# Layer 0 context attention: probabilities turned on VectorE, contexts in row quarters, queries through head queries

## The reference

```
q = split_heads(x @ Wq) * 64 ** -0.5         # 16 heads of 64
k, v = split_heads(context @ Wkv)            # 257 keys a batch, and one null key for all
attn = softmax(q @ k.T)                      # 32 tokens x 258 keys for each batch and head
out = (attn @ v) @ Wout                      # 4096 x 128
out = layernorm(out) * ln_scale + ln_bias ; x = x + out
```

## Time and profile before

| | |
|---|---|
| median of three runs | 4478.43 us |
| span of the profiled execution | 4472.7 us |
| start of the first `scores` / end of the stage's last instruction | 66.47 us / 1493.06 us |
| TensorE busy over the span | 3820.3 us, 85% |
| VectorE / ScalarE / GpSimd busy over the span | 62% / 45% / 18% |

### The profile page before, as it was taken

How to read it: one execution, slowest core, us unless ns; L and a number is a source line. 1 busy time by engine, 2 the same in 40 slices (tenths; PEclk the granted TensorE clock), 3 DMA queues, 4 the chain that set the end, 5 groups by cost and what they waited for, 6 DMA issues and landing times. The chain is left out here.

```text
span 4472.7 us, 86385 instructions
## 1 busy us (share of the span) xinstructions
PE 3820.3 (85%) x31654; PEld 2744.1 (61%) x31654; DVE 2761.5 (62%) x5370; ACT 2025.9 (45%) x4334; POOL 816.0 (18%) x797
## 2 busy tenths in 40 slices
PE   8999999999999772389998779899997777879776
PEld 6777777777777441266676356566664345656454
DVE  5666666666666586522224866577776946878683
ACT  2333333333333455444333344388887745644323
POOL 0000000000000131200000046555552022200160
PEclk9999999999999886789999889999998989989868
DMA  3111111111111055410000032222220000000000
GB/s 110 49 48 48 48 48 48 48 48 48 48 48 53 14 153 163 148 39 0 0 0 26 1 134 114 99 63 68 68 72 23 0 6 3 0 13 0 9 2 24
DMA packets 202958, 216.01 MB, mean 48 GB/s; under 512 B 37280, under 2 KB 190784, under 8 KB 195280
## 3 DMA queue, kind: packets, MB, share of 16 engines
q1 hardware_dynamic: 202704, 212.63, 15.0%
HBM read 185.26 MB, written 27.05 MB: 47 GB/s over the span
## 5 line engine op out<-in xcount | busy, mean ns | idle before, releaser
L3944 PE MATMUL c_psO<-c_pt,c_vc 128*128 128x512 f32 x1024 | 485.5, 596 | 2.5 <-ACT c_ot L4053 2.5
L3916 PE MATMUL c_psS<-c_kc,c_qt 128*128 128x257 f32 x2048 | 465.9, 380 | 1.1 <-DVE c_qt L4092 1.1
L4045 ACT ACTIVATE c_sc<-c_psS,c_mx 128x257 f32<-128x257 f32 x512 | 214.9, 472 | 487.0 <-DVE c_mx L4110 487.0
L3916 PEld LDWEIGHTS c_psS<-c_kc,c_qt 128*128 128x128 f32 x2048 | 381.2, 190 | 67.0 <-issue 17.5
L637 PEld LDWEIGHTS f_psY<-f_w_down,f_hT 128*128 128x128 f32 x2560 | 302.7, 192 | 64.3 <-issue 48.4
L680 ACT ACTIVATE f_hT<-f_psH,f_b_up 128x512 f32<-128x512 f32 x320 | 214.2, 688 | 279.6 <-PE f_psH L627 274.6
L3901 PEld LDWEIGHTS c_psQ<-XT,c_m 128*128 128x128 f32 x1984 | 258.6, 191 | 96.3 <-issue 92.3
L627 PE MATMUL f_psH<-f_xs,f_w_up 128*128 128x512 f32 x640 | 301.7, 607 | 17.6 <-ACT f_hT L680 17.6
L637 PE MATMUL f_psY<-f_w_down,f_hT 128*128 128x128 f32 x2560 | 306.9, 276 | 9.7 <-ACT f_hT L680 5.2
L2320 POOL TENSOR_TENSOR x_sc<-x_sc,x_rec 128x1156 f32<-128x1156 f32 x128 | 270.5, 2113 | 208.4 <-DVE x_rec L2586 208.4
L4053 ACT ACTIVATE c_ot<-c_psO 128x512 f32<-128x512 f32 x256 | 152.9, 597 | 342.6 <-PE c_psO L3944 342.6
(11 more groups left out here) (819 smaller groups left out, 7687.1 us busy)
## 6 DMA issues: line engine op xcount, KB each, us to landing
c_kc<-in_ctxT SPq DMA_DIRECT2D x128, 257.0 KB
c_vc<-in_ctx SPq DMA_DIRECT2D x128, 256.0 KB
g_wide<-g_w_dram SPq DMA_DIRECT2D x32, 1024.0 KB, 8.3
x_kc<-in_ctxT SPq DMA_DIRECT2D x32, 512.0 KB
x_vc<-in_ctx SPq DMA_DIRECT2D x64, 256.0 KB
l_k_dram<-l_dist SPq DMA_DIRECT2D x32, 256.0 KB, 4.0
l_q_dram<-l_turn SPq DMA_DIRECT2D x8, 1024.0 KB, 9.8
y_pt<-l_q_dram SPq DMA_DIRECT2D x8, 1024.0 KB, 6.5
```

Of the source, the lines that this page charges most:

```text
L3916: mm = pe.matmul(psS[:, r, 0:KEYS], qt[:, b // BT, half, b % BT, r * G:(r + 1) * G].rearrange("p h i -> p (h i)"), kc[:, b // 2 % 2, b % 2 ...
L3944: mm = pe.matmul(psO[:], vc[:, slot, c % 2, t, half * P:(half + 1) * P], pt[:, c % 2, t], start=(t == 0), stop=(t == 1))
L4045: act.activation(sc[:, b % 2, r, 0:KEYS], psS[:, r, 0:KEYS], ACT.Exp, bias=mx[:, b % 2, r:r + 1]).then_inc(exp_done, 1)
```

## The change

Four things are altered together:

1. The probabilities are turned by VectorE, with one STREAM_TRANSPOSE of 128 x 1024 (`scale_and_turn`), which turns each 32 x 32 block in its place. The four tokens-by-head quarters of the partitions stay apart, and the keys come to lie 32 to a quarter. The eight TensorE transposes and their two readouts go.
2. The contexts are formed in four row quarters: 64 products of 32 rows, 128 columns each (before 4 of 128 rows, 512 columns), each quarter into a bank of its own. The values of a batch must lie in all four quarters, so they are loaded four times (`values`, 4 DMAs of 256 KB for each batch). S and V read two banks each. The contexts now run one batch behind the scores instead of two.
3. The queries are formed in two steps. `heads` makes head queries (two products of 128 x 128 a batch), S takes them out into `c_qh`, and `fill` multiplies them with the key weights in two row halves of 64 (eight products of 128 columns a batch) into the score banks, right after the exponentials have been taken. S and V read two banks each. `c_m` is not formed any more.
4. The banks are now `c_psA` (scores, queries) and `c_psB` (contexts, head values, head queries, output). `head_values` is spread over four batches, `output` comes one group later, and `att` takes the place of the tokens in `XT`. The loads of `context_weights` are reordered, and the counting of x (bn_stats) moves behind its steps.

```diff
+                def fill(banks, j):
+                    for half in range(2):
+                        for a in range(2):
+                            for e in range(2):
+                                mm = pe.matmul(banks[:, 2 * a + e, half * P:(half + 1) * P],
+                                               w["k"][e * DV:(e + 1) * DV, 2 * j + a, half * P:(half + 1) * P],
+                                               qh[e * DV:(e + 1) * DV, 2 * j + a], start=True, stop=True)
+                    mm.then_inc(q_in, 1)
...
-                def turn(n, b):
-                    pe.wait_ge(scaled, n + 1)
...
+                def context(n, b, count, valued, heads_read, outs_read, opening=False):
+                    pe.wait_ge(turned, n + 1)
+                    pe.wait_ge(vc_loaded[b % 4], count * 64)
+                    pe.wait_ge(heads_ready, heads_read)
...
+                    for half in range(2):
+                        for t in range(KB):
+                            for e in range(G):
+                                mm = pe.matmul(psB[:, e, half * P:(half + 1) * P],
+                                               vc[e * S:(e + 1) * S, b % 4, t, half * P:(half + 1) * P],
+                                               pt[e * S:(e + 1) * S, :, t], start=(t == 0), stop=(t == KB - 1))
...
+                        scores(i, b, first, last)
...
+                        if not (last and s == 1):
+                            pe.wait_ge(heads_ready, n + 2)
+                            pe.wait_ge(exp_done, n * EX + G)
+                            pe.nop(nofuse=True)
+                            fill(psA, b % BT)
+                        if not (first and b == 0):
+                            pe.wait_ge(ot_ready["act"], n)
...
+                            head_values(psB[:, 1], 1 - s, b % BT)
+                        if b % BT == 0 and not first:
+                            output(m - 2, s)
...
+                            heads(psB[:, 0], i * 2 + (b + 1) // BT + 1, (2 * to, 2 * to + 1))
...
+                def scale_and_turn(n, b, first):
+                    v.wait_ge(rec_done, n + 1)
+                    v.tensor_tensor(sc[:, b % 2], sc[:, b % 2], bcast(rc[:, b % 2], 2, NK), ALU.mult)\
+                        .then_inc(scaled, 1)
+                    v.wait_ge(scaled, n + 1)
+                    if not (first and b == 0):
+                        v.wait_ge(context_done, n)
+                    v.transpose(pt[:], sc[:, b % 2, :, 0:KB * S]).then_inc(turned, 1)
...
+                def values(n, slot, fresh):
+                    if not fresh:
+                        sp.wait_ge(context_done, n - 3)
+                    for e in range(G):
+                        sp.dma_start(vc[e * S:(e + 1) * S, slot],
+                                     k.a["ctx"][ds(n, 1), 0:2 * P].rearrange("b (t p) c -> p (b t) c", p=S))\
+                            .then_inc(vc_loaded[slot], 16)
```

More of the change, by code:

```diff
@@ L3599, in free @@
                             pe.wait_ge(taken[e], j - 1)
[L3601 to L3610, removed]
                 pe.wait_ge(o_loaded, 16)
                 pe.wait_ge(v_loaded, 16)
-                for j in range(M_STEPS, W_AT):
-                    half, eight = divmod(j - M_STEPS, 2)
+                for j in range(W_AT):
+                    half, eight = divmod(j, 2)
                     free(j)
@@ L3769, in context_attention, with fills_before @@
         out_read = k.sem("c_out_read")
-        def before(i, b, first):
-            if first and b < BT:
-                return FILLS
-            return (i * 2 + b // BT) * TURNS + FILLS - 2
-        def turns_done(b, at, opening, filling):
-            n = 0
-            for bb in range(b + 1):
-                for aa in range(3 if bb < b else at):
-                    use = TURNS_AT[bb][aa]
-                    if use and not (use[0] == "v" and opening) and not (use[0] == "q" and not filling):
-                        n += 1
-            return n
+        def fills_before(i, b, last):
+            return FILLS if last and b >= BT else i * NB + b + FIRST
         with nc.Block() as block:
@@ L4065, in chunk @@
+                def chunk(i, first, last):
                     for b in range(NB):
+                        n = i * NB + b
+                        m, s = i * 2 + b // BT, b // BT
                         exponentials(i, b, first)
[L4067 to L4070 removed]
                         if not (first and b == 0):
[L4072 removed]
@@ L4073, in chunk @@
-                        if not (first and b < 2):
-                            context(i, b, 1)
-                chunk(0, True)
-                with act.Fori(1, NI) as i:
-                    chunk(i, False)
-                context(NI, 0, 0)
-                copy(B - 1, NB - 1)
-                context(NI, 0, 1)
-                for half in range(2):
-                    context(NI, 1, half)
+                            take_contexts(n - 1, (b - 1) % NB)
+                        if not (last and s == 1):
+                            take_queries(psA, n + FIRST, 1 - s, b % BT)
@@ L4084, in _ @@
+                for j in range(FIRST):
+                    take_queries(psB if j % 2 else psA, j, 0, j)
+                take_heads(3, 0)
+                chunk(0, True, False)
+                with act.Fori(1, NI - 1) as i:
+                    chunk(i, False, False)
+                chunk(NI - 1, False, True)
+                take_contexts(B - 1, NB - 1)
+                output(NG - 2)
                 output(NG - 1)
@@ L4163, in chunk @@
-                        turn_of_bank(0)
-                        turn_of_bank(1)
-                        if not (first and b == 0):
-                            copy(n - 1, (b - 1) % NB)
-                        scale(n, b)
-                        turn_of_bank(2)
-                for j in range(FILLS):
-                    read(psS[:, j % G], j, 0, j)
+                            turn_tail(m - 1, 1 - s)
+                        invert(n, b)
+                        if not (first and b == 0):
+                            take_contexts(n - 1, (b - 1) % NB)
```

402 lines of the change are left out of this document (183 added, 219 removed).

## The result

Four runs of the changed kernel gave 4512.24 to 4519.83 us, median 4516.97, beside 4478.86 for the kernel before: a ratio of 1.0092 [1.0078, 1.0106]. I had forecast 4390, with a range of 4357 to 4465, and slower at 0.12. The span of the profiled execution went from 4472.7 to 4518.0 us, 45.3 more; the medians went up by 38.1. Where both are on record a time lies 1.7 to 2.9 us above its span, so the profiled execution of before was faster than the median, and the 5.7 us that I added in the forecast were mostly scatter.

What follows compares the result with a forecast made beforehand. TensorE, busy 1393 of 1396 us, was taken as the bound. A batch falls from 11.12 to 10.39 us; 120 x 0.73 = 88 off 4472.7 gives 4384.7, plus 5.7 about 4390 us, range 4357 to 4465.

Steps and rivals of the forecast that it cites:

- The steps of the batch: TensorE's parts, us: scores 3.56, contexts 3.70, queries 1.02, head values 1.02, head queries 0.49, output 0.50.
- rival C: Contexts on TensorE: four quarters do not overlap fully, so slower; 4.43 us eats the whole gain; chance 0.12.
- my sum: TensorE's work for a batch after the change, its parts added: 10.29 us, against 11.12 before.
- The ring through the other engines: Scores, exponentials, queries, readout and next scores, linked because queries now use the score banks.
- the 9.0 that I worked out: VectorE's round from one query readout to the next: 9.0 us, against 9.79 of TensorE work without output.
- rival B: VectorE or a readout becomes the round: gain only 0.1 to 0.5 us a batch, 4418 to 4466 us; chance 0.2.
- D: Value loads fall behind and starve the contexts, or the change does nothing: slower or equal; chance 0.03.
- my signs: Wrong if context groups exceed 4.4 us, or TensorE idles for VectorE's `c_qt` or, before contexts, for a DMA.
- The gain of the loop: 0.73 us less for each of 120 batches in full swing, 88 us in all.
- the mean wait of 0.10: Added to each batch for new TensorE waits on readouts: 10.29 to 10.39 us.
- 5 + 2 - 7 = 0: Start and end of the stage together: no net change, with 8 us either way.
- my 4: At the start, the 16 small null loads and the first maxima come some 4 us later.

Runs made afterwards that it cites:

- e6: Changed kernel with two of the eight blocks of 32 keys kept in the contexts, 32 context instructions a batch instead of 128: 4290.4 us.
- e2: Changed kernel with TensorE's hardware loop over blocks of eight batches written out (14 copies): 4434.73 us, ratio 0.9893 to the kernel before.
- e1: Changed kernel with the three loads of `c_wv` and `c_wo` issued before SyncE waits for the null scores: 4503.38 us, ratio 1.0055 to the kernel before.
- e9: e3 with the first two of three value blocks also loaded ahead of the null scores: 4409.51 us, ratio 0.9854 to the kernel before.
- e3: Changed kernel with TensorE's loop written out and `c_wv`, `c_wo` loaded early: 4416.8 us, ratio 0.9863 to the kernel before; its repeat 4422.57 us.
- e10: e9 with TensorE's null scores also put ahead of the first group's head queries, ScalarE's readouts likewise: 4410.42 us, ratio 0.9858 to the kernel before.
- e5: Changed kernel with three of four value loads left out after the first ones: 4501.49 us, ratio 1.0069 to the kernel before.
- e8: Changed kernel with two chunks (16 batches) in TensorE's loop body, run 7 times: 4481.65 us, ratio 1.0018 to the kernel before.
- e4: Kernel before the change with two chunks (16 batches) in TensorE's loop body, run 7 times instead of 14: 4486.17 us, ratio 1.0032.

## Why the prediction was wrong

**The steps of the batch held.** Contexts 3.78 (I took 3.70 and bounds of 3.58 to 4.17 from the earlier trace rows): 128 instructions that start 28.2 ns apart, a quarter of 0.111 within 2%, so rival C is out. The transpose took 1246 ns (1.24 from the two sizes in the earlier trace rows). Queries 1.10 and head queries 0.55 were 0.08 and 0.06 above my sum: over the bare rate, a group in another division costs 0.22 (contexts, queries) or 0.14 (head values), where I took 0.14 for all. The ring through the other engines is not the bound: where TensorE had only 7.7 us of work, plain batches came every 8.6 to 8.8 us (in e6, scores at 626.44, 635.08 and 643.83), less than the 9.0 that I worked out, so rival B is out. No wait of TensorE for value loads stands in the loop, though they keep the engines busy for 0.55 to 0.60 of the time and not 0.43: D, as I wrote it, is out. The idle time did stand before `c_psA<-c_kc,c_qt`, where I had looked for B, but put to issue, which was not among my signs.

**The gain of the loop was mis-sized.** 0.73 a batch times 120 was 88 us. Without pauses it was 63.7. I had 10.39 for a batch, and e2 has 10.54: the changes of division cost more, and the mean wait of 0.10 did not appear. The full gain of 0.57 came in only 112 of the 128 batches: the first block took 80.1 against 79.0, and the last seven batches gained 0.6 together.

**The step that failed** in the loop is one that was not in the sum. I counted instructions for the time that TensorE's array needs for them (16 + 128 + 16 + 16 + 4 a batch), and never asked how many stand in the loop. The trace of before could have warned me: its page has the queue of instruction fetches, and in a round of this loop, 501 to 590 us with its body of 1215 instructions, that queue is silent. 64 products in place of 4 put the body at 3051. Cost: 51.4 us of pauses in TensorE, and the other 27 or so the lower clock behind them, 79 in all. (The clock was granted at 0.50 for 65 us in 13 stretches, one at each pause. Behind the pause at 260.80 a stretch of 3.41 us, from 265.6 on, made 16 score instructions 1.76 us longer. At that rate I estimate some 33 us for the 65, and part of it lies inside the pauses.) The prediction's sentence "There is no gap in it, so every product removed shortens the batch" held for time on the array; products split into quarters nearly keep that time, 3.78 us a batch against 3.44, and multiply the instructions, 128 against 8.

**The second failing step** is "I count 5 + 2 - 7 = 0" for the ends. The sum followed the null scores and missed three moved loads. SyncE's queue was costed only in the loop. I had written "Each load has three batches until it is read"; `c_wv` and `c_wo`, of which the first scores wait, have none. Cost: 30.0 us at the start, of which 13.6 by the medians and 18.9 by the traces came back when the loads were moved (the null loads and the fetches stood behind). The first maxima were 3.1 us later than before (71.97 in e1 against 68.87), near my 4, but the first eight batches took 88.9 to 91.2 us against 79.0 before, where I had counted 5 for the start; with e9's order it was 81.6. The end gave back 2.5 us instead of 7: from the last scores to the next stage's first instruction 32.2 before and 29.7 after, which the later stages' scatter hides in the span.

Together: -63.7 + 79.0 + 30.0 = 45.3, the change of the span.

That nearly all of the 0.12 on the slower side was put on C, the one mechanism that a row could price, made the range too narrow. It had no room for a resource that no row of before shows at work.

## What to carry to other kernels

When a change splits products into more and smaller ones, count the instructions between a hardware loop's start and its end, per engine, and look whether the instruction queue moves data in that loop before and after. Here the loop was free up to 1515 instructions. From 2283 on, each way back cost 2.7 to 6.3 us and mostly a stretch of lower clock, and 1.2 to 1.5 us in the kernel before with its body doubled. Written out, with as many fetches, the same loop had no pause. For each DMA that a diff moves in a queue, find the wait that reads it and everything now issued ahead of it; a wait for all weights ahead of the first product is decided by the last load in the queue, here 30.2 us later.

## What the runs showed of the hardware

- Fetches of instructions stand beside data in the records of the DMA engines: 14 of 16 KB in 501 to 590 us of the changed kernel. Straight-line code stopped too, in the middle of equal instructions: for 2.93 and 3.96 us in e1_early, and for 2.36 to 3.36 in e3 and its repeat. In e1_early the DMA share was 1.16 from 76 us to the first of these pauses and 1.13 in the 9 us from 90 to 99, ahead of the second. With part of the loads issued earlier the share was 0.78 from 76 to 87 us and 0.41 from 90 to 99 in e9, where these pauses were gone; one of 1.22 us was left in e10, with a share of 1.00 from 76 to 85.5. That the share decides it was not tested.
- With four row quarters in turn, instructions of 128 columns started 28.2 ns apart, against 111 for instructions of the full array: 3.94 times as fast. A long run in one quarter alone stands in no trace.
- The pause has a second price. In the changed kernel the clock was granted at 0.50 for 3.41 or 6.83 us at each of the 13, and behind the one shown 16 score instructions lasted 5.40 us instead of 3.64. It was not so after every such pause: behind one of 3.24 us in e5 and one of 2.92 in e8 the clock stayed at 1.00. In e4, whose pauses are 1.2 to 1.5 us, the scores kept their mean of 380 ns. The recorded texts also put the clock in GHz; no trace shows a frequency, only the granted share, 1.00 in the earlier trace rows and 0.50 in these stretches.
- Four loads of 256 KB into 32 partitions each, one behind the other, occupied the engines out of proportion: 119 GB/s at a share of 0.55, where before 48 GB/s took 0.16. The narrow destination alone does not do it: in e5, with one such load a batch, 50 GB/s took 0.18.
